# Graph attention in three half-precision passes: a new order of the first and last turns, and of one pair of stages in the middle

## The reference

```
h = max(layernorm(x), 0)
q, k, v = h @ Wq + bq, h @ Wk + bk, h @ Wv + bv          (split into 6 heads of 64)
probs = softmax(q k^T / 8 + (0 where adj, else -9e15))    (128 x 128 for each head)
out = x + (probs v, heads joined) @ Wf + bf
```

## Time and profile before

| | |
|---|---|
| median of three runs | 481.37 us |
| the profiled execution: time, span | 482.55 us, 480.8 us |
| busy: PE, DVE, ACT, POOL | 462.6, 365.7, 363.3, 300.0 us |
| mean granted TensorE clock | 0.993 |
| chain that ended last: PE, DMA, DVE, ACT, SPq | 78%, 5%, 5%, 4%, 3% |
| one middle group (223.71 to 251.69 us) | 27.98 us |

### The profile page before, as it was taken

One profiled execution on the slowest core, in us unless ns is written; L12 is line 12 of the kernel. 1 busy time (PEld: TensorE's weight loads), 2 busy tenths in 40 slices (PEclk: granted clock), 3 DMA queues, 4 the chain that ended last, 5 costly groups with the idle time before them and its releaser, 6 DMA issues.

```text
span 480.8 us, 12870 instructions
## 1 busy us (share of the span) xinstructions
PE 462.6 (96%) x4454; PEld 272.9 (57%) x4454; DVE 365.7 (76%) x744; ACT 363.3 (76%) x813; POOL 300.0 (62%) x300
## 2 busy tenths in 40 slices
PE   7979989998999999999999999999999999999976
PEld 3744556565465564656556465655646555565653
DVE  5998978796669596776959687695968768577934
ACT  4669997887578886877788687778877778967920
POOL 3095766586666576776657676665767565744760
PEclk9999999999899999999999999999999999999989
DMA  8165797879679698786859778695979969694994
GB/s 297 59 129 127 147 191 141 148 140 207 155 107 229 132 183 203 148 201 130 211 123 204 177 149 204 131 222 112 201 179 170 179 91 195 159 186 85 174 177 132
DMA packets 219663, 78.56 MB, mean 163 GB/s; under 512 B 199520, under 2 KB 219616, under 8 KB 219616
## 3 DMA queue, kind: packets, MB, share of 16 engines
q1 hardware_dynamic: 208992, 65.43, 70.9%
q10 hardware_dynamic: 10624, 12.53, 9.2%
HBM read 16.19 MB, written 12.58 MB: 60 GB/s over the span
## 4 chain that ended last, share of the span: by engine, by line
PE 78%; DMA 5%; DVE 5%; ACT 4%; SPq 3%; issue 2%; POOL 2%; ACTq 0%; DVEq 0%; POOLq 0%
PE ps_proj L927 22%; PE ps_proj L929 22%; PE ps_proj L928 22%; PE ps_scores L1007 6%; DMA ct_parts<-ctx_parts 3%; PE ps_ctx L927 2%; PE ps_ctx L928 2%; PE ps_ctx L929 2%; ACT probs L626 2%; DMA pt_parts<-probs_parts 1%; SPq L469 1%; SPq L477 1%; POOL probs_parts L541 1%; DMA x_sb<-in_x 1%; DVE qkt_lo L740 1%
## 5 line engine op out<-in xcount | busy, mean ns | idle before, releaser
L541 POOL TENSOR_TENSOR probs_parts<-probs,probs_parts 128x768 f16<-128x768 f32 x64 | 105.2, 1644 | 30.0 <-ACT probs_parts L651 29.5
L626 ACT ACTIVATE probs<-masked,neg_max 128x128 f32<-128x128 f32 x384 | 118.4, 390 | 2.7 <-DVE neg_max L766 2.3
L927 PE MATMUL ps_proj<-ht_parts,w_hi 128*128 128x512 f16 (+1 forms) x309 | 109.9, 361 | 2.0 <-issue 1.4
L928 PE MATMUL ps_proj<-ht_parts,w_hi 128*128 128x512 f16 (+1 forms) x309 | 109.8, 361 | 0.0
L929 PE MATMUL ps_proj<-ht_parts,w_lo 128*128 128x512 f16 (+1 forms) x309 | 109.7, 360 | 0.0
L607 ACT ACTIVATE qkt_hi<-ps_proj,bias_qk 128x512 f16<-128x512 f32 x94 | 63.6, 682 | 50.2 <-PE ps_proj L929 49.2
L547 POOL TENSOR_TENSOR ctx_parts<-ctx_sb,ctx_parts 128x384 f16<-128x384 f32 x62 | 56.7, 915 | 55.5 <-ACT ctx_parts L657 55.2
L740 DVE SCALAR_TENSOR_TENSOR qkt_lo<-ps_proj,bias_qk,qkt_hi 128x512 f16<-128x512 f32 x94 | 68.8, 741 | 25.7 <-ACT qkt_hi L607 25.7
L526 POOL TENSOR_TENSOR h_pairs<-h_sb,h_pairs 128x384 f16<-128x384 f32 x60 | 55.8, 937 | 48.1 <-ACT h_sb L598 47.9
L757 DVE SCALAR_TENSOR_TENSOR masked<-ps_scores,score_unscale,mask 128x384 f32<-128x384 f32 x128 | 72.5, 609 | 6.5 <-PE ps_scores L1007 6.4
L536 POOL TENSOR_TENSOR x_bf<-x_sb,b_out 128x384 f32<-128x384 f32 x64 | 63.3, 1001 | 13.3 <-DVE y_sb L789 12.6
(11 more groups left out here) (104 smaller groups left out, 905.7 us busy)
## 6 DMA issues: line engine op xcount, KB each, us to landing
y<-y_sb SPq DMA_DIRECT2D x64, 192.0 KB, 3.0
x_sb<-in_x ACTq DMA_DIRECT2D x56, 192.0 KB, 3.0
x_sb<-in_x SPq DMA_DIRECT2D x8, 192.0 KB, 7.0
pt_parts<-probs_parts SPq DMA_TRANSPOSE x64, 3.9
ct_parts<-ctx_parts SPq DMA_TRANSPOSE x62, 3.0
adj_sb<-in_adj ACTq DMA_DIRECT2D x14, 64.0 KB, 2.8
w_raw<-in_Wq ACTq DMA_DIRECT2D x1, 576.0 KB, 4.7
w_raw<-in_Wf SPq DMA_DIRECT2D x1, 576.0 KB, 6.7
```

The source lines that it names most:

```text
L541: nc.gpsimd.tensor_tensor(probs_parts[b][:, 1, :], probs[b % 2][:], probs_parts[b][:, 0, :], ALU.subtract).then_inc(probs_split, 1)
L626: last = nc.scalar.activation(probs[b % 2][:, u * N:(u + 1) * N], masked[b % 2][:, u, :], ACT.Exp, bias=neg_max[b % 2][:, u:u + 1])
L927: nc.tensor.matmul(to, a_hi, b_hi, start=first, stop=False)
L928: nc.tensor.matmul(to, a_hi, b_lo, start=False, stop=False)
```

## The change

1. **Middle groups.** Three turns of TURNS: `weigh_values(g, 2)` moves behind `project_v(g + 1, 2)`, and `scores(g + 1, 1)` stands right behind it.
2. **Own turns.** All tables of groups 0, 1, 2, 13, 14 and 15 are new, for all five engines. On PE, for instance, `weigh_values(0, 2)` goes behind `project_qk(2, 1)`, and `project_out(2, 1)` ahead of `weigh_values(2, 3)`.
3. **Group 1's normalised graphs** are transposed one by one (`transpose_second`, four DMAs) and not in pairs (two DMAs of `transpose_normed`).
4. **The start.** DVE reduces Wq's rows right behind the first graph's moments. ACT makes `bv_cols` only behind the fourth normalised graph. PE does `project_bias` among the turns, behind `project_qk(0, 3)`.
5. Code for turning probabilities over by PE, which was switched off (PROBS_BY_PE = 0), is gone.

```diff
@@ TURNS (all groups without a table of their own)
-    "scores": (5609, 7804), "mask_scores": (6121, 7156, 8482, 9829), "largest_score": (6841, 7995, 9320, 10570),
+    "scores": (5609, 7814), "mask_scores": (6121, 7156, 8482, 9829), "largest_score": (6841, 7995, 9320, 10570),
...
-    "weigh_values": (12087, 15416, 17087, 18758), "normalize_ctx": (12366, 15695, 17722, 19048),
+    "weigh_values": (12087, 15416, 17802, 18758), "normalize_ctx": (12366, 15695, 17722, 19048),
...
@@ OWN_TURNS: groups 0, 1, 2, 13, 14, 15, all stages
...
-PROLOGUE = {..., "transpose_normed": 1, "normed_lo": 1}
+PROLOGUE = {..., "transpose_normed": 2, "normed_lo": 1}
...
+            def transpose_second(group, b, i):
+                wait(h_split, b + 1)
+                sp.dma_start(ht_parts[1][:, b, :, :], h_parts[b], transpose=True).then_inc(second_h_transposed[b], 16)
...
@@ ACT, written out by hand
             nc.scalar.activation(table_loader[:], eps[:], ACT.Exp)
-            act.wait_ge(bias_loaded, 16)
-            nc.scalar.activation(bv_cols[:], bias_raw[:, 2, :].unsqueeze(2).broadcast_to([P, C, P]), ACT.Copy)\
-                .then_inc(bv_ready, 1)
             normalize_first(0)
...
             normalize_first(3)
+            act.wait_ge(bias_loaded, 16)
+            nc.scalar.activation(bv_cols[:], bias_raw[:, 2, :].unsqueeze(2).broadcast_to([P, C, P]), ACT.Copy)\
+                .then_inc(bv_ready, 1)
             first_hi(2)
...
@@ DVE, written out by hand
             statistics(0, 0, 0)
             first_moments(0)
+            reduce_rows(0)
+            first_shift(0)
             statistics(0, 1, 0)
             first_moments(1)
...
-            first_shift(0)
             statistics(0, 2, 0)
+            statistics(0, 3, 0)
             first_shift(1)
-            reduce_rows(0)
-            statistics(0, 3, 0)
             first_moments(2)
             scale(0)
...
@@ PE
-                if j == 0:
+                if j == 0 and group == 1:
+                    for b in range(B):
+                        pe.wait_ge(second_h_transposed[b], 16)
+                if j == 0 and group >= 2:
                     for pair in range(2):
-                        if group >= 1:
-                            pe.wait_ge(h_transposed[pair], by_group(group - 1, i))
+                        pe.wait_ge(h_transposed[pair], by_group(group - 2, i))
...
             sum_rows(0)
-            project_bias()
             run_turns(pe, {
```

More of the change, by code:

```diff
@@ L74 @@
[L74 to L79, removed]
@@ L80 @@
-        "finish": (22876, 23187, 30388, 30390), "store": (25064, 26171, 28463, 36165), "output_bias": (-6789,),
-        "reduce_output_weight": (13183,), "sum_output_weight": (-1231,), "scale_output_weight": (13199,),
-        "output_weight_hi": (19235,), "split_output_weight": (21291,),
-    },
-    1: {
[L85 to L100, removed]
-    },
@@ L102 @@
-    2: {
[L103 to L108, removed]
-        "values_lo": (10396, 11293, 12646, 16122), "additive_mask": (1080,), "residual": (1508, 1511, 6671, 6672),
-        "scores": (9996, 10695), "mask_scores": (10391, 10394, 11079, 12647),
-        "largest_score": (10392, 10397, 12644, 16054), "exponentials": (10778, 11479, 12172, 16610),
-        "probs_hi": (10780, 12174, 13462, 16611), "probs_lo": (11132, 13951, 13952, 17008),
-        "transpose_probs": (9552, 9553, 16166, 17570), "weigh_values": (14890, 14892, 15611, 19475),
-        "normalize_ctx": (14857, 16120, 17929, 19316), "ctx_hi": (16609, 16613, 17959, 19693),
-        "ctx_lo": (16670, 17009, 18650, 18652), "transpose_ctx": (16172, 19297, 19299, 20373),
-        "finish": (18309, 20886, 24976, 26648), "output_bias": (19827,), "reduce_output_weight": (19965,),
-        "sum_output_weight": (-18673,), "scale_output_weight": (17552,), "output_weight_hi": (19450,),
@@ new lines @@
+        "transpose_normed": (-85576, -59512), "project_qk": (-69816, -69815, -69814, -62708, -36502, -1192),
+        "qk_hi": (-387239, -379006, -1396, -1395, -322, 4612), "qk_lo": (7322, 7479, 7481, 13180, 13181, 13183),
+        "project_v": (-30885, 1305, 1306, 1330), "values_hi": (4304, 9780, 11851, 11852),
+        "values_lo": (13182, 13191, 13196, 15169), "additive_mask": (7480,),
+        "residual": (12511, 14705, 14707, 14711), "scores": (1307, 4922),
+        "mask_scores": (13186, 13187, 21092, 21093), "largest_score": (13189, 13194, 21295, 22875),
@@ new lines @@
+        "exponentials": (13435, 19209, 21958, 21962), "probs_hi": (19208, 19230, 21960, 21963),
+        "probs_lo": (21498, 21500, 21507, 21510), "transpose_probs": (13041, 13234, 25735, 26005),
+        "weigh_values": (29975, 29979, 29987, 29991), "normalize_ctx": (21095, 22873, 23359, 25165),
+        "ctx_hi": (19238, 21959, 24939, 25374), "ctx_lo": (21503, 21506, 23952, 25927),
+        "transpose_ctx": (24845, 24848, 26007, 27568), "project_out": (29981, 29985, 29995, 29997),
+        "finish": (22877, 23187, 25172, 30391), "store": (26003, 26004, 35938, 35940), "output_bias": (6762,),
@@ new lines @@
+        "statistics": (-11123, -10679, -9776, -8555), "aggregate": (-7633,), "inverse_deviation": (-8866,),
+        "shift": (-6381,), "normalize": (-5548, -3980, -3387, -2829), "normed_lo": (-5004, -3732, -3730, -2991),
+        "transpose_normed": (-2887, -2059), "project_qk": (2084, 2085, 2086, 2088, 2089, 4366),
+        "qk_hi": (2386, 3038, 3275, 3277, 3278, 4669), "qk_lo": (1366, 4654, 4691, 4974, 4975, 4977),
+        "project_v": (4368, 6040, 7088, 9475), "values_hi": (4671, 8102, 9532, 9534),
@@ L148 @@
[L148 to L153 removed]
+        "load": (-12261, -11545, -10898, -9594), "load_mask": (-463,), "statistics": (-9113, -9080, -5808, -5806),
@@ new lines @@
+        "statistics": (-15022, -9119, -9115, -5029), "aggregate": (-5026,), "inverse_deviation": (-10245,),
+        "shift": (-5023,), "normalize": (-6257, -6255, -6253, 12628), "normed_lo": (-10242, 42472, 43844, 43845),
+        "transpose_normed": (-383, -166), "project_qk": (-90, -89, 23455, 23456, 23827, 23828),
+        "qk_hi": (12637, 12639, 13336, 13338, 13339, 13340), "qk_lo": (6460, 6462, 6463, 6464, 13411, 13412),
+        "project_v": (26201, 26204, 26207, 59009), "values_hi": (27295, 27301, 35183, 41453),
```

223 lines of the change are left out of this document (106 added, 117 removed).

## The result

The changed kernel takes **477.97 us** (median of 22 runs, 476.4 to 479.83); the kernel before, run beside it, 480.84 us (22 runs, 476.92 to 485.06). Ratio 0.9948, 95% interval 0.9929 to 0.9968. I had forecast 475.0, 6.4 us less than the 481.37 known then; the medians differ by 2.9 us, so the sign is right and most of the gain is missing. The profiled execution took 477.44 us, span 475.7, against 482.55 and 480.8.

A forecast was written before the change was run, and what follows sets the result against it. PE's own stream bounds the middle groups; 10.0 us of waits and half clock behind the start could be won. Terms 0 + 0 - 0.9 - 3.7 + 0 - 3.1 = -7.7 from 482.55 gave 474.9, taken as 475.0; range 470.5 to 481.0.

The forecast's parts named there:

- step 2: Start, up to project_qk(1, 0): 0 us, between -0.5 and +2.8, PE's waits covering the moved project_bias.
- step 6: The end: -3.1 us, bounds 0 and -4.3, from a shorter wait before project_out(14, 2) and no half clock.
- Step 1: Middle groups: same length with the weighting behind project_v, 0 us, bounds -0.1 and +1.0.
- steps 3 and 4: Groups 1 to 3, two shorter PE waits, -0.9 us; around 119 us, two waits and the half clock, -3.7 us.
- Rival D: Middle groups: scores start sooner behind the shorter matmul, 9 x 0.14 = 1.3 us more, 473.7; chance 0.03.
- a transposing DMA of one graph: Group 1's start: half the pair's size, so 2.8 us to its landing, as ctx_parts' row, and not 5.0.
- The Wq chain: Start: reducing Wq's rows earlier on DVE delays the second graph's statistics and, through them, w_lo by 0.6 us.
- The cover for project_bias: Start: PE's waits of 1.08, 0.93 and 1.42 us absorb project_bias's 2.2 us; if not, the price is 2.8.
- Rival B: Slower: the start's cover fails, project_qk(1, 0) behind 39.4, stalls at 119 and 461 stay, 485.3 us; chance 0.08.
- step 4: Around 119 us: -3.7 of 4.1 us, as project_out(2, 1)'s context is issued earlier on SyncE; bounds -4.1 and 0.
- rival A: Waits move on: around 99 to 118 and 447 to 466 us stalls return one stage later, 480 us; chance 0.22.
- Step 5: Groups 12 to 14: tightest inputs still in time, 0 us, bounds 0 to +1.0; sign against it, a new wait there.

The follow-up runs named there:

- e5: Kernel before with the change of the middle groups alone (scores and weigh_values turns): 481.88 us, ratio 1.002.
- e7: Changed kernel with the old orders of groups 13 to 15: 477.28 us, ratio 0.995.
- e1: Changed kernel with project_bias back behind sum_rows(0) and bv_cols back ahead of the first normalised graph: 477.34 us, ratio 0.991.
- e2: Changed kernel with VectorE's hand-written start in the old order, project_bias still among the turns: 478.36 us, ratio 0.996.
- e3: Changed kernel with 9 constant matmuls of unused result added behind sum_rows(0): 480.64 us, ratio 0.998.
- e4: Changed kernel with the whole hand-written start of before (VectorE order, bv_cols, project_bias): 476.74 us, ratio 0.989.
- e12: Same kernel as e4, run again (changed kernel with the whole hand-written start of before): 475.59 us, ratio 0.989.
- e15: Changed kernel with ScalarE's three loads moved later, nothing else: 478.09 us, ratio 0.994.
- e8: Kernel before, unchanged, profiled once more: 479.64 us (one run).
- e13: Kernel before with ScalarE's three loads (x of group 5, mask of group 6) moved behind probs_hi(3, 1), nothing else: 477.91 us, ratio 0.994.
- e14: Same kernel as e10, run again (changed kernel, old hand-written start, three loads later): 474.29 us, ratio 0.989.
- e6: Kernel before with the new orders of groups 13 to 15 alone: 482.03 us, ratio 1.002.
- e11: e12's kernel with the old orders of groups 13 to 15: 475.17 us, ratio 0.988.
- e10: e12's kernel with ScalarE's three loads, whole, moved behind probs_hi(3, 1): 474.05 us, ratio 0.985.

## Why the prediction was right and wrong

The sum failed in three places: in step 2, which put the start at 0 and the clock there at nothing; in step 6, which took 3.1 us from the end; and in the execution from which it subtracted. Step 1 came out, steps 3 and 4 in size.

**Step 1, right.** Period 27.98, eight groups 223.8 us, e5 alone 1.002. Rival D (scores sooner behind the shorter matmul) would have shown 27.84 (27.98 - 0.14) and is out. The Trainium skill, "TensorEngine Tiling (Array Packing)", section Key Properties, says that a change of tiling mode drains the engine; the rows of both profiles and e5 show no gain from a shorter matmul ahead of it.

**Step 2, wrong: 0 forecast, +4.03 us in the profile**, outside my -0.5 to +2.8. Two terms failed. First the clock, which I had put at nothing: I looked for falls where the kernel before had waits, and not where the change made new ones. PE's waits of 1.46, 1.76 and 2.03 us before the first projection brought 6.8 us at half clock. PE was idle in a part of it, so the loss is read between two stages: from the first projection to qk(0, 3) PE took 9.26 us (12.84 to 22.10), before 6.79, so 2.5 us lost; 1.6 in e7 with its one fall. In e1, e2, e3 and e4 this comes back (qk(0, 3) at 18.67 to 19.05). Second, "a transposing DMA of one graph" at the 2.8 us of ctx_parts' row: group 1's four single ones took 3.8 to 4.9 us after, and 4.7, 5.0 and 6.3 (least, median, most) in e12. SyncE issues the four within some 6 us; that they slow each other is not shown. So project_qk(1, 0) could not be at 36.2; with the old start it comes at 36.9 to 37.4, where the kernel before has 36.6 to 37.4. The estimate in the prediction by the Trainium skill, "DMA: Bandwidth & Descriptors", section Anatomy of one DMA, 3.5 us, was nearer and still low against medians of 4.3 and 5.0.

The Wq chain, +0.6 forecast, held: the first projection comes at 12.06 to 12.25 in e7, e15, e1 and e3, which have VectorE's new order (11.82 before). The 12.84 of the profile after is one execution's; there alone VectorE waited 0.46 us for a load of x:

```profile
8.21 1.12 DVE L702 BATCH_NORM_STATS2 stats<-x_sb 128x6 f32<-128x384 f32 x2 [0.46 <-DMA x_sb<-in_x]
```

So of the 4.03 us 1.0 is the late first projection, the larger part of it chance, 2.5 the clock, and 0.5 what is left behind it. The cover for project_bias held too: with the clock up at the start (e2) qk(1, 0) is at 38.08, 0.8 us behind e4. Rival B named this place (decided behind 39.4, and it started at 40.63), but what it foretold next, that the stalls behind it stay, did not come: a late PE finds its data there.

**Steps 3 and 4, right in size and in part for the wrong reason: -4.6 forecast, -5.2 in the profile.** Where the clock falls in neither, the stretch from qk(1, 0) to qk(4, 0) takes 85.8 us in e8 and 81.4 in e12: -4.4. But e4, which is e12's kernel, takes 84.2, and that is only -1.6. With the three loads out of the way in both, e13 takes 85.3, of which 1.7 is its fall (3.4 us at half clock with PE busy), and e14 81.1: some -2.5 by the orders themselves. Of the 4.1 us of step 4 1.7 was a fall that e8 does not have. And project_out(2, 1) came at 119.69, not at 117.6 to 118.5, since the start had made PE late. I took SyncE's queue for the cause of the stall. e13 leaves that queue alone and moves three loads of ScalarE, and most of the stall is gone: it was a collision in flight. In the changed kernel PE, 4 us late, waits 0.52 us there and has little to win (e15); brought to its old time it can lose 2.8 us to it (e4 against e12).

**Step 6, wrong: -3.1 forecast, and the profile agrees for a reason that does not hold.** e6, e7 and e11 say that the end's orders bring nothing: the wait of 2.3 us becomes 0.76 + 1.39, rival A at this place. I had counted 1.7 us for the fall and let the 1.58 us of the second wait stay. The second wait is one execution's: e7 and e8 lack it. The fall came in four of the six profiles with the old end (before, e5, e8, e13; not e7 and e11) and in two of the twelve with the new one (e1, e6), so it did become rarer, and still no median gained.

**Step 5, 0 forecast and in part wrong.** From project_qk(12, 0) to scores(15, 1) it is 99.53 us after against 99.43 before, but 99.96 to 100.54 in seven of the twelve profiles with the new orders (99.43 to 99.65 with the old). That is the new wait before project_qk(14, 5), the sign that the prediction had named for this step; its size stays inside the bound of +1.0 or just past it. It may be what takes back the gain of the rarer fall; no run separates the two.

**The base.** I subtracted 7.7 us from an execution with two falls. The kernel before has none in 14 of 92 runs (478.1) and three or more in 24. And the clock that I read as 1.00 behind the wait of 1.42 us before project_qk(1, 0) was one execution's too: e5, e6 and e13 start as the kernel before does and fall there. Counted from a run without falls, my steps' waits alone (without 1.7 twice) are 4.3 us: 473.8. That the best kernel here has 474.2 is luck, for it has the old start and the moved loads, which I did not foresee, and the end gave none of its 1.4. Of the 3.7 us between it and the changed kernel, 1.4 go with the old start (476.5, median of the eight runs of e4 and e12), the other 2.3 with the three loads, as far as eight and ten runs can tell.

## What to carry to other kernels

Before a stall is written into a sum, see whether it comes in every run: the mean granted clock of each run, set beside its time, says how many falls a run had and what one costs. When work is taken from an engine's wait, ask not only what the wait is worth but what the wait does to the clock behind it. And where a transfer lands late, list what all queues have in flight in those microseconds before the order of its own queue is blamed; here two lines of turns did as much as the whole rearrangement.

## What the runs showed of the hardware

The clock falls behind waits, but not reliably. By place, with the waits ahead of it:

- Before project_qk(1, 0) it fell behind 1.37 us (e11), 1.45 (e13), 2.08 (e5 and e6), 2.10 (e2), 2.25 (e15) and 2.29 (e1), and not behind 1.42 (before), 1.49 (e8), 1.46 (e10), 1.59 (e4), 1.75 (e12) nor behind 2.71 (e3).
- At 121 us it fell behind 1.50 and 0.85 us (before), and not behind 1.52 and 0.93 in the other profile of the same kernel (e8).
- Before project_out(14, 2) it fell behind 2.48 to 2.56 us in four profiles (before, e5, e8, e13) and not behind 2.31 (e7) or 1.90 (e11).
- At the start 1.46, 1.76 and 2.03 us (after) and 1.18 and 2.03 (e15) brought 6.8 us at 1.2 GHz, 0.78, 1.18 and 2.03 (e7) 3.4 us, and a single 2.29 behind short ones (e2) nothing in its profile.

What decides between nearly equal waits stays open.

The same transpose took 3.7, 5.0 and 7.3 us from issue to landing (e10, e12, e4), the last two in one and the same kernel.
